# A graph network's edge pass: block one-hots in float32 with one matmul per tile and part, and gathered rows added by TensorE

## What is computed

```python
# layer 0: for every edge, h = relu(layernorm(x))
edge_input = concat([h[src], edge_attr])                 # 96 + 32 features
messages = gelu(edge_input @ mW1 + mb1) @ mW2 + mb2
gates = sigmoid(gelu(edge_input @ gW1 + gb1) @ gW2 + gb2)
aggregated = segment_sum(messages * gates, dst)
x = x + layernorm(h + mlp(concat([h, aggregated])))
# layers 1 and 2: normalized sum of weight[e] * (x @ W)[src[e]] over the edges of dst, then a gated mix
```

## Time and profile before

| | us |
|---|---|
| median of 3 runs without the profiler (8834.46 to 8851.36) | 8845.47 |
| span of the one profiled execution, its own time (first to last instruction) | 10933.0 |
| of it, edge pass (196 iterations) | from about 133 to about 5800 |
| of it, two convolutions (16 units each) | from about 6120 to 8400, and from about 8500 to 10860 |
| busy in the span: PE | 8192.3 (75%) |
| POOL | 6435.5 (59%) |
| DVE | 4899.6 (45%) |
| ACT | 2690.1 (25%) |

### The profile page before, as it was taken

One profiled execution on the slowest core, in us unless ns is written; L12 is line 12 of the kernel. 1 busy time (PEld: TensorE's weight loads), 2 busy tenths in 40 slices (PEclk: granted clock), 3 DMA queues, 4 the chain that ended last, 5 costly groups with the idle time before them and its releaser, 6 DMA issues. The chain is left out here.

```text
span 10933.0 us, 150076 instructions
## 1 busy us (share of the span) xinstructions
PE 8192.3 (75%) x42144; PEld 5220.9 (48%) x42144; DVE 4899.6 (45%) x11836; ACT 2690.1 (25%) x6600; POOL 6435.5 (59%) x6424
## 2 busy tenths in 40 slices
PE   4777777777777777777777578887777577887776
PEld 4555555555555555555555233333334333433333
DVE  7666666666666666666667122222222121222222
ACT  3444444444444444444443000000000000000000
POOL 4555555555555555555554666666664666666663
PEclk7888888888888888888887788888887688888887
DMA  4444444444444444444444456666565465666656
GB/s 147 123 138 131 136 132 136 132 135 132 135 133 135 133 135 135 134 135 133 135 132 134 155 207 220 216 218 214 208 212 198 156 215 206 224 217 210 210 207 207
DMA packets 933049, 1818.03 MB, mean 166 GB/s; under 512 B 277359, under 2 KB 745600, under 8 KB 875312
## 3 DMA queue, kind: packets, MB, share of 16 engines
q10 hardware_dynamic: 65600, 773.65, 18.6%
q1 hardware_dynamic: 615456, 578.39, 16.9%
q0 software_dynamic: 251856, 464.10, 14.8%
HBM read 1361.12 MB, written 454.48 MB: 166 GB/s over the span
## 5 line engine op out<-in xcount | busy, mean ns | idle before, releaser
L962 POOL DMA_INDIRECT hid<-src_table,src_ids x3127 | 3136.7, 1003 | 2510.4 <-ACT msg L1358 1590.2
L1240 PE MATMUL bd<-ring,table_sb 128*96 128x480 f32 x6272 | 2941.6, 614 | 513.3 <-issue 511.7
L1240 PEld LDWEIGHTS bd<-ring,table_sb 128*96 128x96 f32 x6272 | 1071.7, 176 | 2131.6 <-issue 2131.1
L1007 POOL DMA_INDIRECT hid<-conv_table,hid x1596 | 1561.9, 979 | 751.1 <-issue 486.2
L1155 PE MATMUL sg<-hot,msg 128*98 128x64 f32 x6272 | 831.1, 286 | 1115.9 <-ACT msg L1358 1105.2
L1132 PE MATMUL bd<-one_hot_dst,one_hot_src 128*128 128x168 bf16 (+1 forms) x10368 | 1277.0, 274 | 253.5 <-issue 252.3
L1007 POOL DMA_INDIRECT feat_in<-conv_table,hid x1056 | 1026.1, 972 | 545.2 <-issue 324.6
L1155 PEld LDWEIGHTS sg<-hot,msg 128*98 128x98 f32 x6272 | 746.8, 199 | 1252.2 <-issue 1180.0
L1972 DVE TENSOR_TENSOR acc<-acc,sg 96x64 f32 x400 | 87.2, 218 | 2450.0 <-remote 1652.7
L1132 PEld LDWEIGHTS bd<-one_hot_dst,one_hot_src 128*128 128x128 bf16 x10368 | 1007.1, 110 | 299.1 <-issue 284.3
L1367 ACT ACTIVATE blocks<-bd 128x480 f32<-128x480 f32 (+1 forms) x1152 | 658.1, 571 | 1704.7 <-PE bd L1132 811.8
(11 more groups left out here) (248 smaller groups left out, 10307.8 us busy)
## 6 DMA issues: line engine op xcount, KB each, us to landing
ring<-adjacency ACTq DMA_DIRECT2D x448, 1680.0 KB
adjacency<-blocks SPq DMA_DIRECT2D x384, 980.0 KB
attr<-in_attr SPq DMA_DIRECT2D x392, 128.0 KB
hid<-src_table,src_ids POOLq DMA_INDIRECT x3127
hid<-conv_table,hid POOLq DMA_INDIRECT x1596
feat_in<-conv_table,hid POOLq DMA_INDIRECT x1056
conv_table<-table_sb SPq DMA_DIRECT2D x28, 336.0 KB, 2.4
feat_half<-feat_keep SPq DMA_DIRECT2D x56, 168.0 KB
```

The lines of the kernel that those rows point to most:

```text
L962: pool.indirect_dma_start(out=hid[s][:, t, :], out_offset=None, in_=src_rows, in_offset=bass.IndirectOffsetOnAxis(ap=src_ids[h][:, j:j + 1 ...
L1007: pool.indirect_dma_start(out=conv_g[j][slot][:, t, :], out_offset=None, in_=conv_rows[l], in_offset=bass.IndirectOffsetOnAxis(ap=conv_ids ...
L1240: op = nc.tensor.matmul(side_ps[w].rearrange("r (o z) -> r o z", o=UNIT_OCTETS), table_sb[:, D * k:D * (k + 1)], ring[slot][:, :, OCTET_FA ...
```

## The change

Four things are changed, and nothing outside the edge pass and its constants:

1. The sum of attribute product and gathered rows moves from DVE to PE. `attr_product` leaves its accumulation open, and a new `add_rows` waits for the gathers and adds the rows by two float32 matmuls with the identity (384 columns each) into the same PSUM. DVE's `add` is gone. Gelu reads PSUM and writes `hid[s]`.
2. A part of a block is built by one bfloat16 matmul of zeros over its whole width (which opens the accumulation) and one float32 matmul for each of the four tiles.
3. `y` is one float32 matrix of 128 columns, `z` has 688 float32 columns for every tile; the wide one-hot is gone. `y` is made by a TENSOR_SCALAR with two scalars.
4. The preparation of the sides loses five steps, the split of the weight among them.

```diff
-            side_res = sb_in(edges_phase, "side_res", [P, 5, SIDE_TILES], BF16)
-            side_z = sb_in(edges_phase, "side_z", [P, SIDE_TILES], F16)
+            side_res = sb_in(edges_phase, "side_res", [P, 3, SIDE_TILES], F16)
...
-            y_first = [sb_in(edges_phase, f"one_hot_src0{t}", [P, 3, P], BF16) for t in range(QUAD)]
-            z_s = [[None] + [sb_in(edges_phase, f"one_hot_dst{q}{t}", [P, 2 * Z_PAD], BF16) for t in range(1, QUAD)]
-                   for q in range(2)]
+            y_first = [sb_in(edges_phase, f"one_hot_src0{t}", [P, P]) for t in range(QUAD)]
+            z_second = [sb_in(edges_phase, f"one_hot_dst1{t}", [P, 2 * Z_PAD]) for t in range(QUAD)]
+            iota_z = sb_in(edges_phase, "iota_z", [P, 2 * Z_PAD])
+            zeros_b = sb_in(edges_phase, "zeros_b", [P, P], BF16)
...
-            iota_wide = sb_in(edges_phase, "iota_wide", [P, WIDE_Z], F16)
-            z_wide = [sb_in(edges_phase, f"one_hot_wide{q}", [P, WIDE_Z], BF16) for q in range(2)]
-            iota_lo = sb_in(edges_phase, "iota_lo", [P, P], BF16)
+            z_first = [sb_in(edges_phase, f"one_hot_dst0{t}", [P, 2 * Z_PAD]) for t in range(QUAD)]
+            iota_lo = sb_in(edges_phase, "iota_lo", [P, P])
...
 (attr_product, PE)
                 if free:
-                    pe.wait_ge(s_added, QUADS_PER_ITER * n + s - 1)
+                    pe.wait_ge(s_gelu, QUADS_PER_ITER * n + s - 1)
                 for h in range(2):
                     last = nc.tensor.matmul(
                         attr_ps[s % 2][:, 512 * h:512 * h + 2 * H2], attr[s // 2][:, P * (s % 2):P * (s % 2 + 1)],
-                        w_attr[:, 2 * H2 * h:2 * H2 * (h + 1)], start=True, stop=True)
+                        w_attr[:, 2 * H2 * h:2 * H2 * (h + 1)], start=True, stop=False)
                 last.then_inc(s_attr_mm, 1)
+
+            def add_rows(it, n, s):
+
+                pe.wait_ge(s_gath[s], gathered(it, QUAD, QUAD_SPARED[s]))
+                flat = hid[s][:, :, :].rearrange("p t f -> p (t f)")
+                for h in range(2):
+                    last = nc.tensor.matmul(attr_ps[s % 2][:, 512 * h:512 * h + 2 * H2], ident[:, :],
+                                            flat[:, 2 * H2 * h:2 * H2 * (h + 1)], start=False, stop=True)
+                last.then_inc(s_added, 1)
...
 (build_part, PE)
-                wide = z_wide[q][:, WIDTH * first:WIDTH * (first + m)]
-                nc.tensor.matmul(flat, y_s[q][0][:, 0, :], wide, start=True, stop=False)
-                for k in (1, 2):
-                    nc.tensor.matmul(out[:, :, 0:FAN], y_s[q][0][:, k, :],
-                                     wide.rearrange("p (b w) -> p b w", w=WIDTH)[:, :, 0:FAN], start=False, stop=False)
-                for t in range(1, QUAD):
-                    for k in range(3):
-                        op = nc.tensor.matmul(out[:, :, bass.ds(places[q][t], FAN)], y_s[q][t][:, k, :],
-                                              z_s[q][t][:, z0:z0 + FAN * m].rearrange("p (b d) -> p b d", d=FAN),
-                                              start=False, stop=(t == QUAD - 1 and k == 2))
+                nc.tensor.matmul(flat, zeros_b[:, :], zeros_b[:, 0:1].to_broadcast([P, WIDTH * m]), start=True, stop=False)
+                for t in range(QUAD):
+                    op = nc.tensor.matmul(out[:, :, bass.ds(places[q][t], FAN)], y_s[q][t][:, :],
+                                          z_s[q][t][:, z0:z0 + FAN * m].rearrange("p (b d) -> p b d", d=FAN),
+                                          start=False, stop=(t == QUAD - 1))
                 op.then_inc(s_built, 1)
...
 (edges, PE; in step s, between part 2s and the wait for s_gated)
                     if build:
                         build_part(2 * s, nb, places)
+                    if s + 2 < QUADS_PER_ITER:
+                        add_rows(it, n, s + 2)
+                    elif not last:
+                        add_rows(it + 1, n + 1, s + 2 - QUADS_PER_ITER)
                     pe.wait_ge(s_gated, QUADS_PER_ITER * n + s + 1)
...
 (gelu, ACT)
-                flat = hid[s][:, :, :].rearrange("p t f -> p (t f)")
-                nc.scalar.activation(flat, flat, ACT.Gelu).then_inc(s_gelu, 1)
+                nc.scalar.activation(hid[s][:, :, :].rearrange("p (b t) f -> p b (t f)", b=2),
+                                     attr_ps[s % 2][:, :].rearrange("p (b c) -> p b c", b=2)[:, :, 0:2 * H2],
+                                     ACT.Gelu).then_inc(s_gelu, 1)
...
 (spread_sides, DVE)
-                    place = side_now[:, 4, QUAD * q + t:QUAD * q + t + 1]
-                    if t == 0:
-                        v.tensor_scalar(z_wide[q][:, :], iota_wide[:, :], place, None, ALU.is_equal)
-                    else:
-                        v.tensor_scalar(z_s[q][t][:, :], iota_z[:, :], place, None, ALU.is_equal)
-                    v.scalar_tensor_tensor(out=y_s[q][t][:, :, :], in0=iota_lo[:, :].unsqueeze(1).to_broadcast([P, 3, P]),
-                                           scalar=side_now[:, 0, QUAD * q + t:QUAD * q + t + 1],
-                                           in1=side_now[:, 1:4, QUAD * q + t].unsqueeze(2).to_broadcast([P, 3, P]),
-                                           op0=ALU.is_equal, op1=ALU.mult).then_inc(s_yz, 1)
+                    source, place, weighed = (side_now[:, f, QUAD * q + t:QUAD * q + t + 1] for f in range(3))
+                    v.tensor_scalar(z_s[q][t][:, :], iota_z[:, :], place, None, ALU.is_equal)
+                    v.tensor_scalar(y_s[q][t][:, :], iota_lo[:, :], source, weighed,
+                                    ALU.is_equal, ALU.mult).then_inc(s_yz, 1)
...
 (edges, DVE)
-                    if s + 2 < QUADS_PER_ITER:
-                        add(it, n, s + 2)
-                    elif not last:
-                        add(it + 1, n + 1, s + 2 - QUADS_PER_ITER)
```

More of the change, by code:

```diff
@@ L59 @@
 SETUP_STEPS = 21
-POOL_CONSTANTS = 12
-COUNT_COPIES = 10
+POOL_CONSTANTS = 13
+COUNT_COPIES = 7
 MIX_STEPS = 6
@@ L102 @@
 BANK_Z = tuple(b * FAN + (b >= HALF_BLOCKS) for b in BANK_FIRST)
-WIDE_Z = BLOCKS * WIDTH
 PIECES = 14
@@ L132 @@
 SLICE = SIDE_TILES // SLICES
-ALL_PREP = 35
+ALL_PREP = 30
 UPD_ROWS = D + 3
@@ L217, in build @@
             upd_bottom = sb_in(edges_phase, "upd_bottom", [D, D])
-            iota_z = sb_in(edges_phase, "iota_z", [P, 2 * Z_PAD], F16)
         table_sb = sb("table_sb", [P, BLOCKS * D])
@@ L307, in build @@
         with contextlib.ExitStack() as edges_phase:
-            y_second = [sb_in(edges_phase, f"one_hot_src1{t}", [P, 3, P], BF16) for t in range(QUAD)]
+            y_second = [sb_in(edges_phase, f"one_hot_src1{t}", [P, P]) for t in range(QUAD)]
         buf_b.append(sb("buf_b1", [P, CHUNK]))
-        y_s = [y_first, y_second]
+        y_s, z_s = [y_first, y_second], [z_first, z_second]
         hid_all = sb("hid", [P, QUADS_PER_ITER * QUAD * H2])
@@ L912, in _ @@
             for fill in (lambda: pool.memset(w_attr[:, :], 0.0),
+                         lambda: pool.memset(zeros_b[:, :], 0.0),
                          lambda: pool.memset(ident[:, :], 0.0),
@@ L1141, in edges @@
                 if first:
-                    for s in range(3):
-                        attr_product(n, s, s == 2)
+                    for s in range(2):
+                        attr_product(n, s, False)
+                        add_rows(it, n, s)
+                    attr_product(n, 2, True)
                 for s in range(QUADS_PER_ITER):
@@ L1630, in _ @@
                 do.did(v.tensor_copy(iota_z[:, Z_PAD * (h + 1) - 1:Z_PAD * (h + 1)], count_i[:, 2 * Z_PAD - 1:2 * Z_PAD]))
-            for i0 in range(0, WIDE_Z, 2 * Z_PAD):
-                i1 = min(i0 + 2 * Z_PAD, WIDE_Z)
-                do.did(v.tensor_scalar(iota_wide[:, i0:i1], count_i[:, 0:i1 - i0], float(i0), None, ALU.add))
             assert do.n == COUNT_COPIES
@@ L1654, in dst_quad @@
                 return rel[:, bass.ds(it * TILES_PER_ITER + QUAD * s, QUAD)].unsqueeze(2).to_broadcast([P, QUAD, WINDOW])
-            def add(it, n, s):
-                i = QUADS_PER_ITER * n + s
-                dve.wait_ge(s_gath[s], gathered(it, QUAD, QUAD_SPARED[s]))
-                dve.wait_ge(s_attr_mm, i + 1)
-                pair = hid[s][:, :, :].rearrange("p (b t) f -> p b (t f)", b=2)
-                v.tensor_tensor(pair, attr_ps[s % 2][:, :].rearrange("p (b c) -> p b c", b=2)[:, :, 0:2 * H2], pair,
-                                ALU.add).then_inc(s_added, 1)
             def dot(n, s, first):
@@ L1718, in edges @@
                 if first:
-                    add(it, n, 0)
-                    add(it, n, 1)
                     dot(n, 0, True)
@@ L1747, in edges_start @@
                 wait_apart(dve, s_round[0], r + 1)
-            src_f, dst_e, base_e, q_a, q_b, k_a, low, dl, ok, rest, k_b, c_a, off = (t[:, :] for t in prep)
+            src_f, dst_e, base_e, q_a, q_b, k_a, low, dl, ok, k_b, c_a, off = (t[:, :] for t in prep)
             def by_quad(ap):
```

(12 more changed lines are left out.)

15 lines of the change are left out of this document (7 added, 8 removed).

## The result

| kernel | median us | against before, 95% interval |
|---|---|---|
| before | 8842.58 (8834.46 to 8851.36, 4 runs) | |
| changed | 9296.74 (9291.43 to 9299.86, 4 runs) | 1.0508 [1.0493, 1.0523] |

What follows compares the result with a forecast made beforehand. The prediction took POOL's gathers to bound the edge pass at 21.5 us an iteration; PE would then need 24.9, so +3.4 us x 196 = +666 us on 8845 gives 9511, stated as 9510, range 9000 to 9930.

Steps and rivals of the forecast that it cites:

- What bounds before: Edge pass of the kernel before: bound by POOL's gathers, 21.5 us an iteration in the runs, with DVE close behind.
- all else: Time outside the 196 edge iterations and 32 convolution units: 770 us in the profile, 670 without an estimated 100 for pauses.
- POOL's own price: Edge pass: a gather of 1.002 us plus 0.30 of issue, 1.30 x 16 = 20.9 us an iteration.
- PE's prices: Edge pass on PE: add_rows 1.29 us a step, parts +0.16 and +0.17, a step 5.98, an iteration 23.9.
- the gaps on PE: Edge pass: PE's waits for gathers, Gelu, evacuations and s_gated, 0.25 us a step, 1 us an iteration (0 to 2).
- DVE: Edge pass: adds and old one-hots go, z at 0.65 and y at 0.27 us come; DVE falls to 12.9 an iteration.
- The 5 us that DVE saves are worth nothing: Edge pass: DVE's saving of 5 us an iteration brings no time, beyond the distance it had kept behind POOL.
- Rival A: Edge pass not bound by POOL in the runs, so the change gains: 8490 to 8690, say 8600 us; chance 0.09.
- Rival B: Float32 parts on PE: holes cost full price, 0.18 us a record, 9920 us in all; chance 0.15.
- Rival C: New parts on PE run at the old price, 0.085 to 0.1 us a record: no change, 8845 us; chance 0.04.
- Rival D: On PE, add_rows waits for a late gather, two to three us an iteration more: 9900 to 10100 us; chance 0.06.
- Signs that came out otherwise: Changed kernel's profile: fewer than 2227 gathers in 1000 to 5000, DVE below 50% there, convolution units near 142 us.

Runs made afterwards that it cites:

- experiment 1: The kernel before, profiled once more with no edit: the run took 8850.66 us, its profile spans 8848.8 us.
- experiment 4: The kernel before with 13 gathers an iteration in place of 16, the skipped tiles computed from what the buffer holds: 8557.92 us, 0.967 against before.
- the blocks alone: The changed kernel with the sum of gathered rows back on DVE and the float32 blocks kept: 8734.81 us, 0.9867 against before.

## Why the prediction was right, and where its number was off

**What bounds before.** Right. The iteration in the runs was put at 21.5 and is 21.44 [experiment 1]; POOL bounds it [experiment 4]. The 2.4 and 2.0 us of the earlier trace rows were inferred to be pauses of the profiling, and the second profile doesn't have them. That the 21.5 came out so well is partly luck. A unit of the convolution is 127.4 us in the runs, not 123.5, which is 125 us over 32 units; and all else is 8845 - 196 x 21.44 - 32 x 127.4 = 566 us, not 670. The two errors nearly cancel. With the unit alone put right the same working would have given 20.9 us, and a forecast 125 us higher. POOL's own price was low too: a gather with its issue is 1.34 us in the second profile, not 1.30, and this alone lifts 20.9 to 21.4.

**PE's prices.** Right: a step of 5.98 us was predicted and is measured, with each piece within 0.01; float32 records with holes at 0.141 and 0.147 us, measured 0.1425 and, from (3008.71 - 3007.52)/8, 0.149.

**The term that was off: the gaps on PE, 1 us an iteration** (from 0 to 2 in the prediction). They are 0: PE has no idle time in 3000 us. The term was taken from waits that could come, but all of them were early enough; here the bound engine's partners had slack, and it ran without gaps. With it at 0 the sum would have been 8845 + (23.9 - 21.5) x 196 = 9315, 18 us from the median. Of the error of 213 us this term is 196. The 18 are a difference of two: the iteration grew by 2.48 us, not 2.4, which is 16 us more, and the edge pass grew by 450 us where 2.48 x 196 would be 486. What made the iterations outside 1000 to 4000 cheaper was not taken apart; the first four build no blocks.

**DVE.** z was put at 0.65 us and is 0.574, y at 0.27 and is 0.341: that y lies above both of its bounds, though a 64-column TENSOR_TENSOR takes 0.22 us. DVE is busy for 1665.19/3000 x 23.92 = 13.3 us an iteration, 12.9 predicted; ACT for 12.9, where it was to keep 12.7. "The 5 us that DVE saves are worth nothing" is right for the changed kernel. It is not right for the kernels that POOL bounds: DVE's work has a second price, paid by POOL's instructions. The prediction took POOL's 1.002 us as a constant; 0.945 of it is the gather and the rest comes from what runs beside it.

**Rival A** (not POOL-bound, faster) falls with experiments 1 and 4. **Rival B** (holes cost float32 their full price, 0.18) is wrong: runs of seven columns out of 20 cost a float32 record 0.1425/168 = 0.85 ns a column, as 384 columns without holes do (1.29/4/384 = 0.84). The Trainium skill, page "PSUM — Partial Sum Buffer", section Specifications, says that non-contiguous access patterns slow matmuls significantly; these float32 records do not bear it out. **Rival C** (records at 0.085 to 0.1) is wrong by the same number. Its iteration of 20.5 to 21.5 us was also added up wrongly, 20.1 to 21.0 by the prediction's own prices, with no effect on the forecast. **Rival D** (a late gather holds PE) is wrong: in the view of L1106's line, PE and its weight loads sat idle for late gathers for 17.8 us in the whole pass.

**Signs that came out otherwise.** They were set against the first profile, with its pauses: fewer than 2227 gathers in 1000 to 5000 were expected and 2613 came, and units near 142 us, where they are 127.4 in both kernels. DVE was to stay below 50% there and is at 56%; the prediction's own 12.9 of 24.9 us would have been 52%.

## What to carry to other kernels

Price a change on each engine by starts in the timeline, set that against what the bound needs today, and let the extra count only from where the engine overtakes it: here one half of the change was free and the other was not, and together they cost far more than their sum. When the waits of the new bound all have slack, as here, an allowance for gaps only spoils the sum. And try the parts of a change alone: its float32 blocks are worth keeping, its sum on PE is not. Where POOL's gathers are the bound, look at which of DVE's forms run beside them: a slower form of z made the whole kernel faster.

## What the runs showed of the hardware that was not expected

- **A profiled execution can be 24% longer than the runs, and the next one of the same kernel isn't**: 10933.0 and 8848.8 us. Its pauses hit PE, DVE and ACT, while the median gather stayed at 0.949 us. The granted clock in its edge pass was 0.86 as well, against 0.96 in the second (1000 to 4000).
- **DVE's work lengthens a GpSimd gather, by its form and by where it falls.** A gather takes 0.944 to 0.948 us on average wherever DVE rests through it, counted in every kernel's trace. The mean is 0.999 with the blocks alone, 1.073 with 0.32 us more of DVE a tile, 0.984 with z in a slower form. The changed kernel has 1.031 although its DVE is busy for only 56% of the time, because many of its gathers have a z at the place that hurts. What stays open is the exact rule: which operations cost how much at which place was not tested one by one. y's form made no difference.
- **float32 matmuls write runs of seven columns out of 20 at the rate of columns without holes**, 0.85 ns a column and record against 0.84.
- **PE can run for 3000 us without a gap at a granted clock of 1.00**, with products, sums, two kinds of parts and all their semaphores in one list.
